# A decoder block with state-space layer, cross attention and gated MLP: four places re-ordered, and GpSimd taking a subtraction and a sum of the attention

## What is computed

```python
x = _layernorm(x + _L0_attn_ref(x, ...))     # state-space layer: 128 heads of 64, 8 groups, causal conv of 4 taps
x = _layernorm(x + _L0_xattn_ref(x, ctx_1024, ctx_1024, 0, mask_SxS2_ff0))
x = _layernorm(x + _L0_ffn_ref(x, ...))      # 512 -> 1792 (silu(gate) * up) -> 512, fp16 weights

# cross attention: 32 heads of 16, 8 key/value heads, 128 queries and 128 keys per batch
scores = einsum('bsgrd,btgd->bgrst', xq, xk) / sqrt(16) + mask
out = einsum('bgrst,btgd->bsgrd', softmax(scores), xv)
```

## Time and profile before

| | us |
|---|---|
| runs, median of 3 | 1634.29 (1633.79 to 1634.43) |
| the profiled execution, its own time | 1632.67 |
| its span in the trace | 1630.9 |
| TensorE busy | 1609.1 (99%) |
| VectorE busy | 1192.2 (73%) |
| GpSimd busy | 975.8 (60%) |
| ScalarE busy | 945.8 (58%) |
| mean granted clock of TensorE | 0.999 |

### The profile page before, as it was taken

How to read it: one execution, slowest core, us unless ns; L and a number is a source line. 1 busy time by engine, 2 the same in 40 slices (tenths; PEclk the granted TensorE clock), 3 DMA queues, 4 the chain that set the end, 5 groups by cost and what they waited for, 6 DMA issues and landing times.

```text
span 1630.9 us, 25574 instructions
## 1 busy us (share of the span) xinstructions
PE 1609.1 (99%) x9096; PEld 1268.2 (78%) x9096; DVE 1192.2 (73%) x2370; ACT 945.8 (58%) x1578; POOL 975.8 (60%) x741
## 2 busy tenths in 40 slices
PE   9999999999999999999999999999999999989998
PEld 7788888888888888888888888888888885444646
DVE  7767687767877686868685868586858689996443
ACT  6765377446835583648373837383728565994231
POOL 4977478656956594849493949385938573331000
PEclk9999999999999999999999999999999999999999
DMA  5432133212412231314231414132404245000000
GB/s 206 143 104 82 55 105 135 78 60 92 135 59 91 87 129 56 104 59 136 69 114 45 136 59 136 46 116 79 136 13 136 91 86 129 1 21 20 16 12 26
DMA packets 73570, 138.83 MB, mean 85 GB/s; under 512 B 6786, under 2 KB 10882, under 8 KB 73092
## 3 DMA queue, kind: packets, MB, share of 16 engines
q1 hardware_dynamic: 73444, 137.21, 26.2%
HBM read 132.98 MB, written 2.63 MB: 83 GB/s over the span
## 4 chain that ended last, share of the span: by engine, by line
PE 92%; DVE 5%; issue 1%; DMA 1%; ACT 0%; POOL 0%; SPq 0%; DVEq 0%; POOLq 0%; ACTq 0%
PE ps_hs L249 8%; PE ps_hs L251 8%; PE ps_hs L250 8%; PE ps_gate L250 8%; PE ps_gate L249 8%; PE ps_gate L251 8%; PE ps_y L1220 7%; PE ps_hs L1229 7%; PE ps_hs L1230 7%; PE ps_hs L1228 7%; PE ps_gate L1204 4%; PE ps_y L1513 3%; PE ps_hs L1438 3%; PE ps_dec L1438 3%; DVE pr L1052 2%
## 5 line engine op out<-in xcount | busy, mean ns | idle before, releaser
L799 DVE SCALAR_TENSOR_TENSOR conv<-ps_hs,cw,conv 128x508 f32<-128x508 f32 (+2 forms) x432 | 320.0, 741 | 31.5 <-ACT conv L566 20.3
L400 POOL TENSOR_TENSOR cum_bc<-cum_bc,neg_cum 128x1024 f32<-128x1024 f32 x128 | 247.5, 1934 | 10.8 <-DMA cum_bc<-cum_scratch 0.2
L249 PE MATMUL ps_hs<-x_hi,w_hi 128*128 128x512 f32 x576 | 231.5, 402 | 0.0
L251 PE MATMUL ps_hs<-x_hi,w_lo 128*128 128x512 f32 x576 | 225.2, 391 | 0.0
L249 PE MATMUL ps_gate<-x_hi,w_hi 128*128 128x512 f32 x576 | 224.4, 390 | 0.0
L250 PE MATMUL ps_hs<-x_lo,w_hi 128*128 128x512 f32 x576 | 224.4, 390 | 0.0
L250 PE MATMUL ps_gate<-x_lo,w_hi 128*128 128x512 f32 x576 | 224.3, 389 | 0.0
L251 PE MATMUL ps_gate<-x_hi,w_lo 128*128 128x512 f32 x576 | 224.2, 389 | 0.0
L1228 PE MATMUL ps_hs<-wo_hi,g_hi 128*128 128x512 f32 x488 | 190.5, 390 | 0.0
L1230 PE MATMUL ps_hs<-wo_hi,g_lo 128*128 128x512 f32 x488 | 190.0, 389 | 0.0
L1229 PE MATMUL ps_hs<-wo_lo,g_hi 128*128 128x512 f32 x488 | 190.0, 389 | 0.0
(11 more groups left out here) (177 smaller groups left out, 3327.6 us busy)
## 6 DMA issues: line engine op xcount, KB each, us to landing
cum_bc<-cum_scratch SPq DMA_DIRECT2D x128, 512.0 KB, 4.1
w_raw<-w_in SPq DMA_DIRECT2D x145, 256.0 KB, 4.6
wo_raw<-w_out SPq DMA_DIRECT2D x64, 256.0 KB, 4.8
g_acc<-x_t SPq DMA_DIRECT2D x4, 512.0 KB, 5.6
acc<-x_nat SPq DMA_DIRECT2D x1, 2048.0 KB, 9.2
out<-y_out SPq DMA_DIRECT2D x8, 256.0 KB, 2.0
wg_sb<-w_gate SPq DMA_DIRECT2D x1, 1792.0 KB, 7.0
wu_sb<-w_up SPq DMA_DIRECT2D x1, 1792.0 KB, 11.0
```

The source lines that it names most:

```text
L249: eng.matmul(ps, whi, xhi, start=(k == 0), stop=False)
L251: return eng.matmul(ps, wlo, xhi, start=False, stop=(k == n - 1))
L400: gp.tensor_tensor(part, part, start.broadcast_to([P, 2, HB, SEQ]), ALU.add).then_inc(S["bc_ok"], 1)
L799: v.scalar_tensor_tensor(out=dst, in0=src, scalar=cw[:, at, TAPS - 1 - n:TAPS - n], in1=dst, op0=ALU.mult, op1=ALU.add).then_inc(S["tap"], 1)
```

## The change

Four places and two moved operations:

1. *Prologue.* GpSimd waits for dt_dve to reach 2 + BATCH, which the eight scans count up, before split(2).
2. *First queries.* TensorE's order was the products of batches 4 and 5, turn_queries(0), batch 6, scores(0), batch 7. It becomes batch 4, turn_queries(0), batch 5, scores(0), batch 6, batch 7. VectorE's second_part(6) and first_part(7) move between the two halves of masked(0).
3. *x2.* The second powers come in three calls: batches 0 and 1 at GpSimd's i == 20, 2 and 3 at i == 27, 4 to 7 behind the casts. x2_high stands behind the exponentials of par 0, x2_low behind masked(i, 1). batch_done comes a step later, in the MLP at m == 1 for batch 6 and m == 3 for batch 7.
4. *Last product.* The last batch's 28 products of 512 columns become 2 x 28 of 256, into ps_gate[0] and [1]; VectorE adds and takes statistics of one half at a time, and combines them at the end.
5. *GpSimd.* less_max(i) subtracts neg_max, broadcast along the row, from the four heads of par 1 in one instruction, and ScalarE's exponentials of par 1 become one instruction of 512 columns without a bias. add_attended(n) does the sum L1075 on GpSimd. ScalarE's keep_turned_too takes par 1 of the odd chunks, so VectorE copies only those of even chunks.

```diff
...
             gp.tensor_tensor(dt_u, dt_v, a_col[:, 0:1].broadcast_to([P, TOK]), ALU.mult).then_inc(S["dt_pool"], 1)
+            pool.wait_ge(S["dt_dve"], 2 + BATCH)
             split(2)
...
-            def powers(stage, cols):
+            def powers(stage, n, cols):
...
                     .then_inc(S[f"eps{stage}"], 1)
-                pool.wait_ge(S[f"eps{stage}"], 1 + (cols.stop == BATCH))
+                pool.wait_ge(S[f"eps{stage}"], n + 1)
                 gp.tensor_tensor(rstd[stage - 1][:, cols], rstd[stage - 1][:, cols], minus_half[:, cols], ALU.pow)\
                     .then_inc(S[f"pow{stage}"], 1)
+            def add_attended(n):
+                b, o = n // 2, n % 2
+                pool.wait_ge(S["att_ok"], n + 1)
+                cols = slice(o * 256, (o + 1) * 256)
+                gp.tensor_tensor(acc[:, b, cols], acc[:, b, cols], att[:, o, :], ALU.add).then_inc(S["xa_ok"], 1)
+            def less_max(i):
+                pool.wait_ge(S["s_max"], 2 * i + 2)
+                part = pr[i % 3][:, REP:2 * REP, :]
+                gp.tensor_tensor(part, part, neg_max[:, i % 3, REP:2 * REP].unsqueeze(2).broadcast_to([P, REP, SEQ]),
+                                 ALU.subtract).then_inc(S["sub_ok"], 1)
...
                 if i == 4:
-                    powers(1, slice(2, HB))
+                    powers(1, 0, slice(2, HB))
                 if i == 9:
-                    powers(1, slice(HB, BATCH))
-                if i == 25:
-                    powers(2, slice(0, HB))
+                    powers(1, 1, slice(HB, BATCH))
+                if i == 20:
+                    powers(2, 0, slice(0, 2))
+                if i == 27:
+                    powers(2, 1, slice(2, HB))
+                if i >= 2:
+                    less_max(i - 2)
+                if i % 2 == 0 and i >= 10:
+                    add_attended((i - 10) // 2)
+            less_max(CHUNKS - 2)
+            less_max(CHUNKS - 1)
+            for n in range(CHUNKS // 2 - 5, 2 * BATCH):
+                add_attended(n)
             pool.wait_ge(S["acc_ok"], BATCH * GROUPS)
...
                 gp.tensor_copy(wd_sb[:, m, :], wd_raw[:, m % 2, :]).then_inc(S["wd_ok"], 1)
-            powers(2, slice(HB, BATCH))
+            powers(2, 2, slice(HB, BATCH))
...
-                act.wait_ge(S["s_max"], 2 * i + par + 1)
+                if par:
+                    act.wait_ge(S["sub_ok"], i + 1)
+                    part = pr[i % 3][:, REP:2 * REP, :].rearrange("p r t -> p (r t)")
+                    sc.activation(part, part, ACT.Exp, scale=-1.0).then_inc(S["p_exp"], 1)
+                    return
+                act.wait_ge(S["s_max"], 2 * i + 1)
                 for r in range(REP):
-                    n = par * REP + r
+                    n = r
                     e = sc.activation(pr[i % 3][:, n, :], pr[i % 3][:, n, :], ACT.Exp, scale=-1.0,
...
                 sc.activation(pr_t[i % 3][:, 0, :], ps_gate[0][:, :], ACT.Copy).then_inc(S["pt_a"], 1)
+            def keep_turned_too(i):
+                act.wait_ge(S["pt_ps"], 2 * i + 2)
+                need(act, S["pt_v"], i)
+                need(act, S["pv_ps"], 2 * (i - 3) + 2)
+                sc.activation(pr_t[i % 3][:, 1, :], ps_gate[1][:, :], ACT.Copy).then_inc(S["pt_v"], 1)
...
                     keep_queries(i // KD + 1)
+                if i - 1 < CHUNKS:
+                    exponentials(i - 1, 0)
+                if i >= 4 and i % 2 == 0:
+                    keep_turned_too(i - 3)
                 if i in X2_STEPS:
                     x2_high(X2_STEPS.index(i), BACK_PS)
-                if i - 1 < CHUNKS:
-                    exponentials(i - 1, 0)
                 if i % 2 == 0 and i >= 6:
...
             first_part(6)
-            first_part(7)
-            second_part(6)
             dve.wait_ge(S["m3_neg"], 1)
...
                 dve.wait_ge(S["pt_ps"], 2 * i + 2)
+                need(dve, S["pt_v"], i)
                 need(dve, S["pv_ps"], 2 * (i - 3) + 2)
...
                                 rec[:, o].broadcast_to([P, REP, REP, AD]), ALU.mult).then_inc(S["att_ok"], 1)
-                dve.wait_ge(S["att_ok"], n + 1)
-                cols = slice(o * 256, (o + 1) * 256)
-                v.tensor_tensor(acc[:, b, cols], acc[:, b, cols], att[:, o, :], ALU.add).then_inc(S["xa_ok"], 1)
...
-                attended(b, 1)
                 dve.wait_ge(S["xa_ok"], 2 * b + 2)
...
             for i in range(CHUNKS + 3):
-                if i >= 3:
+                if i >= 3 and (i - 3) % 2 == 0:
                     keep_turned(i - 3)
...
                     if i == 0:
+                        second_part(6)
+                        first_part(7)
+                    masked(i, 1)
+                    if i == 0:
                         second_part(7)
...
                         x2_low(X2_STEPS.index(i), BACK_PS)
-                    masked(i, 1)
                 if i + 2 < BATCH:
...
                     n = (i - 8) // 2
-                    if n % 2:
-                        batch_done(n // 2)
-                    else:
-                        attended(n // 2, 0)
+                    attended(n // 2, n % 2)
+                if i % KD == 3 and i >= 11:
+                    batch_done((i - 11) // KD)
                 if (i + 1) % KD == 0 and (i + 1) // KD + 1 < BATCH:
...
                     normed(1, b, acc[:, b, :]).then_inc(S["x1_ok"], 1)
-                if i == 23:
-                    dve.wait_ge(S["pow2"], 1)
+                if i in (23, 27):
+                    dve.wait_ge(S["pow2"], 1 + (i == 27))
                 if i + 2 in X2_STEPS:
...
                         attended(BATCH - 1, 0)
+                    if m == 1:
+                        batch_done(BATCH - 2)
                     if m == 2:
+                        attended(BATCH - 1, 1)
+                    if m == 3:
                         batch_done(BATCH - 1)
                     if m == 4:
-                        dve.wait_ge(S["pow2"], 2)
+                        dve.wait_ge(S["pow2"], 3)
                     if m in (4, 5):
...
                     dve.wait_ge(S["x2_ok"], n + 1)
-                    v.tensor_tensor(acc[:, n, :], acc[:, n, :], ps_y[n % 2][:, :], ALU.add).then_inc(S["r_ok"], 1)
-                    dve.wait_ge(S["r_ok"], n + 1)
-                    row_stats(3, n)
+                    if n == BATCH - 1:
+                        for c in range(2):
+                            cols = slice(c * HID // 2, (c + 1) * HID // 2)
+                            dve.wait_ge(S["dn_ps"], n + c + 1)
+                            v.tensor_tensor(acc[:, n, cols], acc[:, n, cols], ps_gate[c][:, cols], ALU.add)\
+                                .then_inc(S["r_ok"], 1)
+                            dve.wait_ge(S["r_ok"], n + c + 1)
+                            v.bn_stats(half_stats[:, c, :], acc[:, n, cols]).then_inc(S["st3"], 1)
+                        dve.wait_ge(S["st3"], n + 2)
+                        v.bn_aggr(mv[2][:, n, :], half_stats[:, :, :]).then_inc(S["mv3"], 1)
+                    else:
+                        v.tensor_tensor(acc[:, n, :], acc[:, n, :], ps_y[n % 2][:, :], ALU.add).then_inc(S["r_ok"], 1)
+                        dve.wait_ge(S["r_ok"], n + 1)
+                        row_stats(3, n)
                     variances(3, n, slice(n, n + 1))
...
             pe.wait_ge(S["ss_diag"], BATCH * GROUPS)
-            last_products((4, 5), range(TPH))
+            last_products((4,), range(TPH))
...
             turn_queries(0)
+            last_products((5,), range(TPH))
+            pe.wait_ge(S["gacc_ok"], kept + 2)
+            scores(0)
             pe.wait_ge(S["gacc_ok"], kept + 3)
             last_products((6,), range(TPH))
-            pe.wait_ge(S["rstd_v"], GROUPS)
-            scores(0)
             pe.wait_ge(S["gacc_ok"], kept + 4)
...
                     need(pe, S["r_ok"], n - 1)
+                    if n == BATCH - 1:
+                        for c in range(2):
+                            cols = slice(c * HID // 2, (c + 1) * HID // 2)
+                            for m in range(MT):
+                                for part, hh in enumerate((h_hi, h_lo)):
+                                    mm = pe.matmul(ps_gate[c][:, cols], hh[:, m, b * SEQ:(b + 1) * SEQ],
+                                                   wd_sb[:, m, cols],
+                                                   start=(m == 0 and part == 0), stop=(m == MT - 1 and part == 1))
+                            mm.then_inc(S["dn_ps"], 1)
+                        continue
                     for m in range(MT):
```

3 lines of the change are left out of this document (2 added, 1 removed).

## The result

The changed kernel takes 1639.52 us (median of 9 runs, 1637.43 to 1640.77), the kernel before, run beside it, 1633.79 us (9 runs, 1632.42 to 1634.81). The ratio is 1.0034, with a 95% interval of 1.0025 to 1.0043: 5.7 us slower, by more than the 0.2% that can be told from no change. The forecast was 1638.6 us (+4.3), range 1633 to 1644. The profiled execution took 1639.52 us with a span of 1637.5 (before 1632.67 and 1630.9), +6.6 in the span.

What follows compares the result with a forecast made beforehand. TensorE was taken as the bound, so other engines' gains count only where it waits. The terms -1.5 + 0 - 5.8 + 10.4 + 1.8 - 0.6 = +4.3 us, carried to the runs' median 1634.29, gave 1638.6 us, range 1633 to 1644.

Steps and rivals of the forecast that it cites:

- prologue: First 60 us: with L373 behind the scans the slow scan loses 2.15 us, and TensorE's waits shrink: -1.5 us.
- first queries: At turn_queries(0): TensorE waits some 1.5 us for normed, made good while VectorE is the late one: 0, +-0.5.
- steady attention: Chunks 12 to 24: the other engines fall under TensorE's 11.9 us per four chunks, its 2.4 us of waits go: -2.5.
- x2 stretch: Of 5.0 us of TensorE waits the first 1.6 go, and some 1.7 of the last 3.4 stay: -3.3 us.
- late power: Before x2's batch 4 transposes: the power behind the casts ends at 1509.65, so TensorE waits 9.75 us.
- wait for h_f(5): Behind batch 4's transposes: hidden(7) needs the buffer h_f(5) frees at 1511.35, making the stall 10.4 us.
- lower clock behind the stall: After the stall: some 4 us of TensorE work at half speed, +1.8 us, bounds 0 and +2.8.
- last product: Kernel's end: 256-column halves at 0.1135 us each, shorter sum and statistics behind them: -0.6 us, bounds -0.7 and +0.8.
- the GpSimd order: Last sums, casts, power: five add_attended ahead of the 14 casts, second power behind them; the casts' earlier cover is gone.
- the hold: Shared-port rival: VectorE held through GpSimd instructions in the attention, +2 to 3 us, 1641 us; chance 0.08.
- 0.62: Chance of the forecast case: a stall of 10 to 11 us and a gain of 5 to 9 before it.
- the rival with casts that aren't late: Before batch 4's transposes: casts run back to back in 8.2 us, no stall or clock loss, 1628 us; chance 0.09.

Runs made afterwards that it cites:

- The filled stall: The changed kernel with 46 additional unread products ahead of the transposes of x2's batch 4: 1637.51 us, ratio 1.0023 to the kernel before.
- the kernel without a stall: The changed kernel with GpSimd's last powers (batches 4 to 7) ahead of the 14 casts: 1626.23 us, ratio 0.9953 to the kernel before.

## Why the prediction was right, and where its terms were not

Its direction, its cause and its place held: TensorE stands at the transposes of batch 4 because the power stands behind the 14 casts, which stand behind the last sum. Moving one call took the whole loss away. Term by term, in us, from the two traces:

| term | forecast | measured |
|---|---|---|
| prologue | -1.5 | -1.5 |
| first queries, to chunk 3 | 0 | +0.9 |
| chunks 3 to 12 (not in the sum) | 0 | -0.9 |
| steady attention, chunks 12 to 24 | -2.5 | -2.67 |
| x2 stretch | -3.3 | -2.6 |
| late power, to batch 4's transposes | +9.75 | +10.49 (10.34 idle) |
| wait for h_f(5) behind them | +0.65 | +0.5 |
| lower clock behind the stall | +1.8 | +2.6 |
| last product | -0.6 | -0.16 |
| sum | +4.3 | +6.7; the span has +6.6, the medians +5.7 |

The stall was right by its parts: the sum took 0.73 us (forecast 0.65), the casts 1482.89 to 1501.87, 18.98 (forecast 18.5 from before's 19.0), the power 1.36 (1.34), the first normalisation some 0.7 later the transposes. That 10.4 was forecast and 10.34 us of idle time measured is partly luck: the 10.4 held 0.65 for h_f(5), which does not show as a wait of its own, since at half clock hidden(7) came late enough, and the casts were 0.5 us longer than taken. The filled stall shows the 0.5 of h_f(5). That the casts lose their cover when sums are put ahead of them is what the GpSimd order showed.

**The clock term** was mis-sized. I took some 4 us of work at half clock, from the warm-up matmuls; it was 6.1 us (1503.92 to 1510.0). Half of that is 3.05; less the 0.5 that h_f(5) would have cost at full clock too it is 2.6, and filling the stall gave 2.58. With +2.6 in the sum the forecast would have been 1639.4.

**The first queries** were a step that failed though its 0 came out. I said that TensorE's wait of 1.4 us (measured 1.43) is made good while VectorE is the late one. It is not: the chunks' chain on VectorE starts from scores(1), and that start moved by the wait. By position the changed kernel is 0.6 us ahead at chunk 3, where the prologue alone would make it 1.5, so part 2 cost 0.9 there (1.1 when tried alone, 1.65 for the part without second_part(7)'s new place). By chunk 12 it is 1.55 us ahead: the lighter VectorE gained 0.9 in between, which I had not counted. Two errors of opposite sign; the old order keeps the gain without the cost.

**The x2 stretch** kept 3.0 us of waits instead of 1.7. Up to 0.9 of these can come from the pair L1027, which takes 1.85 us in place of 1.00 beside GpSimd's k_bd and subtraction (the duration is shown, its share in the wait for att only argued). I had the hold among the rivals, at 2 to 3 us and with a chance of 0.08; it was there, and its price was not measured, but the whole stretch fell only 0.7 us short of the forecast. The Trainium skill (SBUF — State Buffer, "Who interferes with whom") has the rule for a VectorE instruction in a two-port mode, that the one that comes first keeps the pair of ports for its whole instruction; the ends 0.28 us behind GpSimd's and the run without the subtraction (0.97 for the pair) agree.

**The last product** lost on the pitch, 0.120 us instead of 0.1135. Nor did I read the price row right: the 1.95 us of 16 products of 128 columns hold the 0.275 us of the last one, so that from start to start it is (1.95 - 0.275) / 15 = 0.11, not 0.12. It gave no bound for 256 columns, and half of the pitch of 512 was too little by 0.0065 us, 56 times.

**The steady stage** was right, cause and size: TensorE as the bound at 35.60 / 3 = 11.87 us per four chunks (forecast 11.9). That GpSimd stays under it is confirmed, with 2 us of slack.

**Two slips in the working** did not touch the forecast. "About a third" of 0.62 lies below 1637.6, but the chances took 0.25 of it, four tenths. And the rival with casts that aren't late was given a remainder of 1.6 us for h_f(5), while its own numbers, 1501.0 against 1500.90, give 0.1. Without it that rival says 1626.4, and the kernel without a stall took 1626.23.

The difference between +6.6 in the traces and +5.7 in the medians is mostly that the profiled execution of the kernel before, 1632.67 us, lay 1.1 below the median of its runs; the rest is within what the first 40 us vary between executions.

## What to carry to other kernels

When an engine that had slack is given work in one stage, look at what stood behind in its queue: here the sums cost nothing where they ran, and 13.3 us through a power that had been parked behind 14 transfer-bound casts as long as these were early. Put what others wait for ahead of bulk work, and then price a stall with the clock behind it: a 10 us wait cost 13. A wait on an engine that isn't the bound yet is only made good if the chain that is the bound does not start behind it.
